# Layer 2 of a four-layer graph network written out in order, panels of block 0 moved to the end, block ends counted in groups

## The reference

```python
h = layernorm(x)                                     # each of layers 0 to 2
# layer 0: relational sum
x += segment_sum((h @ weight[type])[src], dst) + segment_sum(edge_attr, dst) @ ... + h @ loop_weight + bias
# layer 1: mean of the source rows
x += linear(concat(h, segment_mean(h[src], dst)))
# layer 2: a hidden layer on every edge
m  = relu(concat(h[src], h[dst], edge_attr) @ W1 + b1)   # 200000 x 128
x += segment_sum(m @ W2 + b2, dst)  combined with  h @ Wn + bn
# layer 3: linear again, output
out = x + linear(concat(x, segment_sum(x[src], dst)))
```

## Time and profile before

| | us |
|---|---|
| median of 3 runs | 7200.89 (7191.73 to 7232.2) |
| the profiled execution's own time | 7163.53 |
| its span in the profile | 7161.7 |
| granted TensorE clock, mean | 0.743 of 2.4 GHz |
| busy: PE, PEld, DVE, ACT, POOL | 4714.0, 3020.3, 2438.5, 2060.6, 3998.2 |
| layer 0 / 1 / 2 / 3, from the clearing of `acc` to the next | 2462 / 921 / 2705 / 819 |

### The profile page before, as it was taken

The page is one execution under the profiler, slowest core; times in us unless marked ns, Lnnn a source line. Parts: engine busy times, 40 slices in busy tenths (PEclk is TensorE's granted clock), DMA queues, the critical chain, the costliest instruction groups (busy, mean ns, idle before and its releaser), DMA issues. The chain is left out here.

```text
span 7161.7 us, 86379 instructions
## 1 busy us (share of the span) xinstructions
PE 4714.0 (66%) x24800; PEld 3020.3 (42%) x24815; DVE 2438.5 (34%) x6392; ACT 2060.6 (29%) x3761; POOL 3998.2 (56%) x4125
## 2 busy tenths in 40 slices
PE   6565665666676656888646666666666666668885
PEld 3343443333333332344435554455545555533433
DVE  6443343333443333434222222222222222234232
ACT  5333333333566550010112222222222222210000
POOL 0466666666666555655246665555555555546653
PEclk8656567677666677888667887777777777778886
DMA  5433333332333335655222222222222222245562
GB/s 212 148 70 71 73 77 77 78 80 76 103 105 110 99 98 178 210 199 199 66 54 63 64 64 60 61 62 60 59 59 58 60 59 58 60 144 203 191 206 74
DMA packets 626790, 724.54 MB, mean 101 GB/s; under 512 B 235557, under 2 KB 526858, under 8 KB 607084
## 3 DMA queue, kind: packets, MB, share of 16 engines
q1 hardware_dynamic: 427578, 506.86, 21.5%
q0 software_dynamic: 130976, 185.66, 11.7%
q10 hardware_dynamic: 67986, 28.96, 1.5%
HBM read 518.59 MB, written 201.58 MB: 101 GB/s over the span
## 5 line engine op out<-in xcount | busy, mean ns | idle before, releaser
L1117 POOL DMA_INDIRECT layer_msg<-snd_table,layer_idx x1565 | 1480.3, 946 | 1305.7 <-DMA rel_table<-first_rows 442.8
L1128 POOL DMA_INDIRECT layer_msg<-rel_table,idx_rel x1536 | 1556.7, 1013 | 840.0 <-issue 420.9
L1811 PE MATMUL layer_sum_ps<-layer_sel,layer_msg 128*128 128x128 f32 (+14 forms) x8192 | 1139.7, 292 | 986.3 <-issue 445.8
L1835 PE MATMUL layer_unit_ps<-layer_frame_hot,layer_low_hot 128*128 128x350 bf16 (+9 forms) x3792 | 1111.5, 440 | 758.9 <-ACT layer_frames L1348 425.6
L1811 PEld LDWEIGHTS layer_sum_ps<-layer_sel,layer_msg 128*97 128x97 f32 (+2 forms) x8192 | 1069.4, 209 | 1161.1 <-issue 638.6
L1348 ACT CAST layer_frames<-layer_unit_ps 128x700 fp8e4<-128x700 f32 (+9 forms) x1268 | 953.1, 785 | 1341.0 <-remote 539.0
L1128 POOL DMA_INDIRECT layer_msg<-h_table,idx_src x896 | 849.9, 949 | 658.5 <-issue 238.5
L1851 PE MATMUL layer_panel_ps<-layer_piece,layer_pairs 128*128 128x504 fp8e4 (+9 forms) x3920 | 953.8, 399 | 124.6 <-issue 84.5
L1835 PEld LDWEIGHTS layer_unit_ps<-layer_frame_hot,layer_low_hot 128*128 128x128 bf16 x3792 | 395.3, 124 | 1310.4 <-issue 614.0
L1522 DVE TENSOR_TENSOR layer_msg<-layer_pre_ps,layer_msg 128x512 f32<-128x512 f32 x392 | 270.3, 690 | 1128.6 <-remote 696.0
L1851 PEld LDWEIGHTS layer_panel_ps<-layer_piece,layer_pairs 128*128 128x128 f16 x3920 | 391.2, 103 | 622.1 <-issue 253.5
(11 more groups left out here) (236 smaller groups left out, 3780.6 us busy)
## 6 DMA issues: line engine op xcount, KB each, us to landing
layer_piece<-counts SPq DMA_DIRECT2D x48, 1575.0 KB
layer_attr<-in_edge_attr_dram SPq DMA_DIRECT2D x790, 64.0 KB
rel_table<-first_rows SPq DMA_DIRECT2D x98, 512.0 KB, 2.7
layer_piece<-counts SPq DMA_DIRECT2D x24, 1500.0 KB
layer_piece<-counts SPq DMA_DIRECT2D x16, 1593.8 KB
layer_rcv<-rcv_table SPq DMA_DIRECT2D x396, 64.0 KB
layer_msg<-snd_table,layer_idx POOLq DMA_INDIRECT x1565
layer_piece<-counts SPq DMA_DIRECT2D x16, 1543.8 KB
```

The source lines that it names most:

```text
L1117: nc.gpsimd.indirect_dma_start(msg[g][:, u, 0:2 * D if dense else width], None, of, bass.IndirectOffsetOnAxis(ap=idx_slot[g][:, u:u + 1], ...
L1128: nc.gpsimd.indirect_dma_start(msg[g][:, u, 0:2 * D if dense else width], None, of, bass.IndirectOffsetOnAxis(ap=idx[:, at:at + 1], axis=0 ...
L1811: last = nc.tensor.matmul(sum_ps[g % 2][0:sums, 0:span], msg[g][:, u, c0:c1], sel[j][:, u, 0:span], start=n_part == 0, stop=n_part == len( ...
L1835: last = nc.tensor.matmul(unit_ps[unit % 2][:, half * 512:half * 512 + cols], low_hot[k % HOT][:, 2 * (r % 2) + v, :], frame_hot[j][:, v, ...
```

## The change

1. **Layer 2 is written out** on every engine like layer 0: 384 groups with the node parts of blocks 0 to 12 between them, then the last 8 groups and block 13 through `run`. POOL gathers straight from `idx_src`; the small index transfers and POOL's waits for them go (but for the last 8 groups). SP loads the attributes and the receiver rows of a group by `load_attr_group` and `load_rcv_group`, with 8 bases per `load_ordered`. Every one-hot keeps its full 128 columns. Between the written-out part and `run`, DVE loads `first` and makes the one-hots of three groups again.
2. **`BLOCK_ENDS` counts groups**, not iterations: 107, 151, 184, 212, 237, 259, 279, 298, 316, 333, 349, 364, 379, where 112, 152, 184, 216, 240, 264, 280, 304, 320, 336, 352, 368, 384 stood. The setup's test of the data follows.
3. **The order of the panels** is `SEQUENCE`: panels 3 to 19, then 0, 1, 2, which hold the edges of block 0 alone (the test of the data asks for that). Blocks now begin at steps 20, 28, 43, 48, 53, 64, 74, 79 (blocks 1, 2, 9, 3, 4, 5, 6, 7), 33, 58, 69, 84 (blocks 8, 10, 11, 12) and 89 (block 0). The last panel has 44 frames where it had 20. In layer 0, block 12 begins at 379.
4. **`low_hot`** in layer 0 compares with `window_iota`, which lies in PSUM, instead of `iota` in SBUF.
5. **A wait moves**: in layers 0, 1 and 3 DVE waited, ahead of `run`, until all stores of the written-out blocks had landed (`stored`). Now it waits at the head of `nodes`, behind the last 8 groups.

```diff
-BLOCK_ENDS = (14, 19, 23, 27, 30, 33, 35, 38, 40, 42, 44, 46, 48, 49)
+BLOCK_ENDS = (107, 151, 184, 212, 237, 259, 279, 298, 316, 333, 349, 364, 379)
+LATE = 3
+SEQUENCE = list(range(LATE, len(PANELS))) + list(range(LATE))
...
-                ends = min(BLOCK_ENDS[b] * PER, DENSE_1)
-                ready = PIECES * (2 + min(k for k, panel in enumerate(PANELS) if panel[0] + panel[1] >= ends))
+                ends = min(BLOCK_ENDS[b], DENSE_1)
+                needed = [k for k, n in enumerate(SEQUENCE) if PANELS[n][0] < ends and (b == 0 or n >= LATE)]
+                ready = PIECES * (2 + max(needed))
...
-                if mlp:
-                    with pool.Fori(0, load_passes(pool)) as p:
-                        with pool.Fori(0, ITERS - 1) as i:
-                            for g in range(PER):
-                                gather(p * ITERS + i, g)
...
+                for q in range(NG):
+                    gather_group(q)
...
+                def load_rcv_group(q, base):
+                    sp.wait_ge(pre_ready, q + 1)
+                    sp.dma_start(rcv[q % SLOTS][:, :], table[1][bass.ds(base, P), :]
+                                 ).then_inc(rcv_in[q % PER], 16)
...
+                if mlp:
+                    for q in range(NG):
+                        if q % PER == 0:
+                            bases = load_ordered(SP_ENGINE, q)
+                        load_attr_group(q)
+                        load_rcv_group(q, bases[q % PER])
...
-                            iota[:, :].unsqueeze(1).to_broadcast([P, TILES, P]), ALU.is_equal)
+                            window_iota.unsqueeze(1).to_broadcast([P, TILES, P]), ALU.is_equal)
...
                 def nodes(b, m):
+                    dve.wait_ge(stored, 16 * stores * (static_blocks + 1))
                     for part in range(PARTS):
...
                 if mlp:
-                    for g in range(3):
-                        select(0, 0, g)
+                    for q in range(3):
+                        select_group(q)
+                    for q in range(LAST_STEP):
+                        if q % PER == 0 and q < NG:
+                            next_bases = load_ordered(DVE_ENGINE, q)
+                        if q < NG:
+                            add_sender(q // PER, q % PER)
+                        if q + 3 < NG:
+                            select_group(q + 3)
+                        if 0 < q <= NG:
+                            add_sums((q - 1) // PER, (q - 1) % PER, bases[(q - 1) % PER])
+                        if q % PER == 0 and q < NG:
+                            bases = next_bases
+                        if q in part_at:
+                            if part_at[q][0] == 0:
+                                dve.wait_ge(acc_added, min(q, NG) + 2)
+                            node_part(*part_at[q])
...
-                    dve.wait_ge(stored, 16 * stores * (static_blocks + 1))
...
                 if mlp:
-                    flip(0, 0)
-                    flip(0, 1)
-                    hidden(0, 0)
+                    flip_group(0)
+                    flip_group(1)
+                    hidden_group(0)
+                    for q in range(LAST_STEP):
+                        if q in part_at:
+                            node_part(*part_at[q])
+                        if q + 2 < NG:
+                            flip_group(q + 2)
+                        if q + 1 < NG:
+                            hidden_group(q + 1)
+                        if q < NG:
+                            sum_up(q // PER, q % PER)
```

155 lines of the change are left out of this document (81 added, 74 removed).

## The result

The changed kernel takes 6957.2 us (median of 4 runs, 6941.6 to 6967.5) where the kernel before takes 7196.3 (4 runs, 7176.1 to 7232.2): a ratio of 0.9677, 95% interval 0.9652 to 0.9702, 3.2% faster. Forecast were 6945 us and a ratio of 0.9644.

The account below looks back on a forecast made before the run. It took chains to bound the kernel, in layer 2 the gathers and their pauses. Layers 2, 0, 1 and 3 gave -210 - 19 - 20 - 6 = -255 us, ratio 0.9644, 6945 us; 8 in 10 from 6740 to 7110.

Parts of the forecast that it names:

- Layer 2, -210 forecast: Writing layer 2 out was to save 220 us, taken as 210 for the seam's uncertainty.
- 384 x 6.21: Layer 2's 384 written-out groups at layer 0's pace of 6.21 us each, node parts included: 2385 us.
- The seam: Between layer 2's written-out part and its loop: register loads of 4.6 us and some 6 to refill the chain.
- Rival B: Layer 2's loop held the gathers up, by DVE's register loads and SP's index transfers; total -385 to -600 us; 15%.
- C: Rival: layer 2's node parts cost nearly what they did, 11 to 17 us per block; total -45 to -125; 17%.
- D: Rival, slower: parts met in fixed order can each cost a pause; 7305 us at 5.5 us a part; 4%.
- Layer 1, -20 forecast: Layer 1's shorter tail, more last frames, block among the panels and moved wait: -20 us (-40 to 0).
- +10: In layer 1, the block leaving the tail lies among the panels, where PE is the limit: 10 us longer.
- -28 + 8 - 10: Layer 1's end: 2.8 blocks left in the tail (-28 us), 24 more frames (+8), moved wait (-10).
- Layer 3, -6 forecast: Layer 3: tail 1.2 blocks shorter (-12 us), frames +8, moved wait -2.4; sum -6 (-15 to +5).
- Layer 0, -19 forecast: Layer 0: block 12 begun among the last groups (-14 us) and low_hot from PSUM (-5); -40 to 0.
- The price of `low_hot`: In layer 0, one-hots reading SBUF slow the gathers, about 20 us; reading PSUM was to save 5 (0 to 20).

Follow-up runs that it names:

- order0b: The changed kernel with the panels in their old order (LATE = 0), on a chip of the slower kind: 6887.1 us against 7186.0 before, ratio 0.9590.

## Why the prediction held, point by point

- **What bounds layer 2** was read wrongly for this chip. The prediction says that the gathers and their pauses set the pace, with POOL's 5.0 us as floor. But POOL pauses because all eight buffers are full (75 groups gathered, 67 summed), so the pause is an effect and not the cause. That PE is not the limit was taken from 2.98 us a group with no gathers left; beside gathers the same engines take 5.8, and how the one comes to slow the others no run shows. The reading fits kind B, where the buffers are empty and half the gathers cut the layer by 31%. What paces layer 2 on kind A stays open. The forecast could still be right because its number was not built on this reading: it took the pace of layer 0, the nearest written-out code on the same chip.
- **Layer 2, -210 forecast, -266 measured.** That the written-out form has layer 0's pace and no full holes was right. The mis-sized term is "384 x 6.21": it measured 6.09 a group (2333.5 us), mostly because layer 2 slows down less towards its end (its last 96 sums come at 6.26 us each, those of layer 0 before the change at 6.57) and starts faster (the first 96 at 5.85 against 6.05); that is 45 us. The seam was as forecast: 11.2 us from the last written-out sum to the first sender add (4.6 and 6 forecast), 25.6 for the last eight groups (24), so the 10 us taken off for its uncertainty come on top. Extra time around a block's parts was (2333.5 - 383 x 5.83) / 13 = 8 us (11 forecast).
- **Rival B's second reason was true, its size not**: SP's index transfers, with the waits that go with them, did hold the groups up, by 0.32 us a group in block 0 (6.15 against 5.83) and 81 us in the layer, where B needed 385 to 600 in all. Its first, DVE's register loads, is not needed for the pace of block 0, which came back whole without them. C and D: the parts cost 8 us a block, no more; neither came.
- **Layer 1, -20 forecast, +39 measured, the step that failed.** The term that failed is "+10" for the block that moves in between the panels: the part ahead of the last addition grew by 69 us. The terms behind it, -28 + 8 - 10 = -30, measured -30. Of the 69, 16 are there with the new block ends and the old order (780.6 against 764.4 us into the layer, `order0b`) and 53 come with the order. The tail (2.8 blocks of 24 us) and the moved wait (14.55 to 4.95) were read rightly; of the 30 us, 10 are the wait and 23 the new block ends, and the new order shortened nothing there. What makes the order cost 53 us is open but for the 7 in panel 0's steps.
- **Layer 3, -6 forecast, +13 measured:** the same step; against the old order 29 us lie ahead of the last addition, none of them with the frames of panels 0 and 1, and 7 behind it.
- **Layer 0, -19 forecast, -8 measured.** Block 12 took 22.5 us out of the end and put 14.4 among the groups (25 and 11 forecast), which is the -8. The gathers went from 1014 to 993 ns, but here POOL waits for free buffers anyway, and the waits grew instead. The price of `low_hot` was bounded by 0 and 20; on kind B, where POOL doesn't wait, it measures 30, on kind A nothing that stands out of the spread between traces (35 us).
- **The total** was right by luck in part, by errors of opposite sign: -56 us in layer 2, +59 in layer 1, +19 in layer 3, +11 in layer 0.

## What to carry to other kernels

Moving work from a serial tail to a stream is worth only what the stream has to spare: here the changed order of the panels cost 53 us ahead of the tail in layer 1 and gained nothing in the tail that the new block ends had not, and taking it back alone gave 0.9%. Test two parts of a change apart before crediting either. A test that takes work out shows what it costs at its place, not what moving it cost; look at the old place too (21 small adds with their loads took 13 us on DVE beside 6 of PE at both). And where a queue of buffers lies between a producer and the rest, count how many are full before you call the producer the limit: empty ones mean that the rest waits for it, and a hole in the rest can be caught up; full ones mean that the rest is the limit, and every hole counts. That decided here whether writing layer 2 out was worth 10% of the layer or nothing.

## What the runs showed that was not expected

The same kernel takes 7200 us on some chips (at least two in these runs) and 5723 on others (two), and the change is worth 3.2% on the former and nothing on the latter. In layer 2 the difference is in who waits: on the first kind the eight buffers are full, POOL stops for 1.9 to 2.8 us behind about eight gathers, and DVE and ACT come out of their waits for PE's signals just before it goes on; on the second the buffers are empty and POOL never stops. PE's granted clock is lower on the first (0.81 against 0.93 in layer 2 of the changed kernel, 0.83 against 0.97 in layer 1's panels, where PE is busy for 597 us of 774 against 530 of 575), so of the 199 us there 67 are PE's own work. Whether the clock also stands behind layer 2's late signals is not shown. What makes the chips differ isn't shown by any trace here and stays open; how much of layer 2's gain on the first kind comes from the spread of the parts and how much from the loop's registers stays open too.
